# Two joints of an attention and mixture-of-experts kernel: the last batches' weight traffic and key copies, and the first gather of the expert block

## The chip, the cores and the metric

The program runs on one core of a Trainium2 chip. A time is the device time of one execution in microseconds (us). The profile is one more execution, recorded by the hardware profiler: every time inside it counts from the start of its span. TensorE is called PE here, VectorE DVE, ScalarE ACT, GpSimd POOL, and SyncE SP. SP computes nothing; it issues transfers. ACT and POOL can issue transfers too.

## What is computed

A layer with cross-attention (32 batches of 112 tokens, 512 channels, 16 heads, 375 context rows) and a mixture of 8 experts, of which each token takes its best 2. Cut to what matters:

```python
x = x + xattn(layernorm(x), ctx, mask, ...)         # q and output projections on int8-rounded operands
h = layernorm(x)
probs = softmax(h @ router_w.T); vals, idx = top_k(probs, 2); vals = vals / vals.sum(-1)
for e in range(8):                                  # 3584 tokens, hidden width 352
    gate, up = split(h @ gate_up[e].T); y = silu(gate) * up @ down[e].T
    out += combine[:, e] * y
return x + out
```

## The kernel before, in words

Three blocks run one after another, and all engines meet at a barrier between them.

**Attention** (lines 18 to 912). Iteration `it` computes the scores and softmax of batch `it`, head by head (h = 0 to 15), and beside them prepares batch n = it + 1 (keys, values, queries), finishes batch m = it - 1, and stores batch m2 = it - 2. The order on each engine is written out by hand in a `body(it, ...)` for that engine. Iterations 3 to 28 are a hardware loop; -1 to 2 and 29 to 33 are written out. Iteration 31 (B - 1) is the last with scores; it has no next batch to project, so PE has little to do there. Iteration 32 (`late`) finishes batch 31, iteration 33 stores it.

Keys and queries must be copied into "stacks" (`k_stack`, `q_stack`) before PE can use them. SP issues these copies: 12 for heads 8 to 15 (`stack_keys(1)`, at the start of an iteration, after the last score of the one before), 12 for heads 0 to 7 of the next batch (`stack_keys(0)`), then 12 for its queries. In iterations 0 to 2 two of the 12 copies of `stack_keys(0)` are issued by ACT instead (`ACT_KEYS`).

In each iteration one of 32 slices of the expert weights is split in a high and a low part, so that the expert block can load them: SP loads the slice into `w_raw` (lines 197 and 198, after the four stores of the slice before have landed: `w_stored`), ACT makes the high part `w_hi` after the softmax of head 12 (line 439), POOL makes the low part in place (`w_lo`, line 329), and SP stores both (lines 245 and 246, four transfers) at the end of its iteration. All of these are in the tile `w_raw_hi`.

In iterations 31 and 32 DVE also does the routing of the first 30 batches (lines 496 to 700), between the heads.

**Routing** (`route`). A long chain on DVE ends in `gather` (line 1124) and `scatter` (line 1126): for each of 63 tiles of 128 slots the rows of `h2` to be gathered and where their results go. Meanwhile SP loads expert 0 (`load_expert`, 8 transfers, 4.3 MB), writes a zero block and stores the weights by token (`weights_by_token`); it waits for both before it leaves the block.

**Experts** (`experts`). For each tile t POOL copies a column of `gather` to `gather_idx` (line 1233), gathers 128 rows of `h2` with an indirect transfer (line 1237), gathers the weights of the tokens (`cw_rows`, line 1250), and later scatters the results (line 1245). PE transposes the rows of tile t + 1 (line 1348) and multiplies them by the expert's weights (lines 1324 and 1357). SP loads expert 1, then counts `weights_ready` up for expert 0, and so on. PE waits for `weights_ready` before the first product of a tile.

## Time and profile before

| | |
|---|---|
| median of 3 runs | 1551.54 us (1551.52 to 1556.08) |
| the profiled execution | 1553.85 us |
| its span | 1552.1 us |
| PE busy | 1484.4 us, 96% of the span |
| DVE, ACT, POOL busy | 889.0, 881.5, 635.5 us |

In the page's 40 slices of the span (38.8 us each) PE is busy for nine tenths or more in all but the first, the last, and slices 28 and 29. Those two hold the end of attention, the routing block and the start of the experts. A row of the timeline gives the start, the duration, the engine with the line, what was written from what, and in brackets how long the engine had sat idle and what released it. An engine name with q (SPq, POOLq, ACTq) is the queue of instructions that issue transfers or count.

### The profile page before, as it was taken

How to read it: one execution, taken by the hardware profiler on the slowest of the kernel's cores; microseconds unless marked ns; L12 is line 12 of the kernel's file. 1: busy time of each engine (PE TensorE's matmuls, PEld its weight loads, DVE VectorE, ACT ScalarE, POOL GpSimd, SP SyncE). 2: the span in 40 equal slices, each digit the busy share in tenths (PEclk: the TensorE clock that was granted, in tenths of full speed). 3: DMA queues.
4: the chain of work that ended last, by engine and by line, in shares of the span. 5: the costliest groups of instructions: out<-in, count | busy, mean ns of one | idle time of the engine just before them, and what ended most of it. 6: DMA issues, size and time to landing. Idle time of an engine off the chain costs nothing. (4 is left out here: it accounts for less than half of the span.)

```text
span 1552.1 us, 40193 instructions
## 1 busy us (share of the span) xinstructions
PE 1484.4 (96%) x11596; PEld 1310.6 (84%) x11597; DVE 889.0 (57%) x2402; ACT 881.5 (57%) x2100; POOL 635.5 (41%) x663
## 2 busy tenths in 40 slices
PE   6999999999999999999999999995599999999996
PEld 5888888888888888888888888874599999999995
DVE  7667766667766676676766667668422222222221
ACT  4776767776777776776777776663133333333332
POOL 3234333344333433334333343323255555656553
PEclk9999999999999999999999999996699999999998
DMA  8676677776777767777677766763647775574743
GB/s 265 180 208 181 179 207 213 214 190 183 218 202 211 188 181 216 202 210 191 182 217 202 214 188 183 204 171 127 215 78 189 189 193 145 123 186 82 189 79 48
DMA packets 220123, 281.08 MB, mean 181 GB/s; under 512 B 83568, under 2 KB 164976, under 8 KB 220080
## 3 DMA queue, kind: packets, MB, share of 16 engines
q1 hardware_dynamic: 202608, 246.32, 56.4%
q0 software_dynamic: 16128, 33.30, 11.7%
q10 hardware_dynamic: 1344, 0.92, 0.3%
q8 instruction: 23, 0.38, 0.1%
q14 instruction: 20, 0.16, 0.0%
HBM read 118.31 MB, written 66.17 MB: 119 GB/s over the span
## 5 line engine op out<-in xcount | busy, mean ns | idle before, releaser
L362 ACT ACTIVATE probs<-probs,neg_max 112x375 f32<-112x375 f32 x512 | 312.1, 610 | 197.2 <-DVE neg_max L536 191.9
L536 DVE CUSTOM_DVE_ANT_0 probs<-score,neg_mask 112x375 f32<-112x375 f32 x504 | 275.3, 546 | 228.0 <-PE score L749 223.3
L757 PE MATMUL turn<-ident,probs 112*125 112x112 f32 x1536 | 262.8, 280 | 3.7 <-ACT probs_t L349 2.6
L349 ACT ACTIVATE probs_t<-turn 125x336 f32<-125x336 f32 x512 | 225.7, 441 | 68.1 <-PE turn L757 67.5
L757 PEld LDWEIGHTS turn<-ident,probs 112*125 112x125 f32 x1536 | 225.9, 189 | 36.0 <-issue 15.7
L749 PE MATMUL score<-k_stack,q_stack 96*112 96x376 f32 x496 | 200.6, 404 | 3.8 <-DMA q_stack<-q_lo 2.0
L304 POOL TENSOR_TENSOR q_tok<-q_tok,bq_row 112x512 f32<-112x512 f32 x32 | 41.8, 1306 | 361.7 <-DVE q_tok L643 361.7
L791 PE MATMUL proj<-ctx_hi,wk_hi 128*128 128x376 f32 x512 | 176.5, 345 | 10.7 <-DVE ctx_lo L714 10.5
L791 PE MATMUL proj<-ctx_lo,wk_hi 128*128 128x376 f32 x512 | 171.9, 336 | 0.0
L791 PE MATMUL proj<-ctx_hi,wk_lo 128*128 128x376 f32 x512 | 171.4, 335 | 0.0
L1287 DVE TENSOR_TENSOR a_lo<-a_ps,a_hi 128x384 fp32r<-128x384 f32 x63 | 35.2, 558 | 237.8 <-ACT a_hi L1262 218.6
L796 PE MATMUL proj<-wv_hi,ctx_hi 128*125 128x512 f32 x384 | 151.6, 395 | 0.0
L796 PE MATMUL proj<-wv_hi,ctx_lo 128*125 128x512 f32 x384 | 151.2, 394 | 0.0
L796 PE MATMUL proj<-wv_lo,ctx_hi 128*125 128x512 f32 x384 | 151.1, 394 | 0.0
L1245 POOL DMA_INDIRECT out<-y_rows,scatter_idx x63 | 101.8, 1616 | 79.3 <-issue 30.0
L324 POOL TENSOR_TENSOR ctx_lo<-ctx_stage,ctx_hi 128x1504 fp32r<-128x1504 f32 x31 | 106.6, 3437 | 38.0 <-ACT ctx_hi L434 37.6
L329 POOL TENSOR_TENSOR w_raw_hi<-w_raw_hi 128x1056 fp32r<-128x1056 f32 x32 | 78.9, 2465 | 88.7 <-ACT w_raw_hi L439 88.7
L791 PEld LDWEIGHTS proj<-ctx_hi,wk_hi 128*128 128x128 f32 x512 | 97.1, 190 | 17.5 <-ACT ctx_hi L447 10.1
L1275 ACT ACTIVATE y_rows<-y_ps,row_share 128x512 f32<-128x512 f32 x63 | 43.4, 689 | 106.9 <-PE y_ps L1357 61.8
L791 PEld LDWEIGHTS proj<-ctx_lo,wk_hi 128*128 128x128 f32 x512 | 97.5, 191 | 0.0
L791 PEld LDWEIGHTS proj<-ctx_hi,wk_lo 128*128 128x128 f32 x512 | 96.7, 189 | 0.0
L362 ACT ACTIVATION_READ_ACCUMULATOR probs<-probs,neg_max 112x1 f32 x512 | 95.6, 187 | 0.0
(244 smaller groups left out, 3339.2 us busy)
## 6 DMA issues: line engine op xcount, KB each, us to landing
k_stack<-x_and_k SPq DMA_DIRECT2D x762, 94.0 KB, 2.4
ctx_stage<-ctx_t SPq DMA_DIRECT2D x32, 750.0 KB, 5.1
q_stack<-q_hi SPq DMA_DIRECT2D x250, 56.0 KB, 2.0
w_raw_hi<-gate_up_t SPq DMA_DIRECT2D x32, 352.0 KB, 3.1
gate_up_dram_hi<-w_raw_hi SPq DMA_DIRECT2D x32, 352.0 KB, 5.3
gate_up_dram_lo<-w_raw_hi SPq DMA_DIRECT2D x32, 352.0 KB, 5.6
gate_up_hi<-gate_up_dram_hi SPq DMA_DIRECT2D x16, 704.0 KB, 4.8
gate_up_lo<-gate_up_dram_lo SPq DMA_DIRECT2D x16, 704.0 KB, 9.6
```

The lines of the kernel that those rows point to most:

```text
L304: pool.tensor_tensor(q_tok[:, :], q_tok[:, :], W["bq_row"][0:N, :], ALU.add).then_inc(q_biased, 1)
L324: pool.tensor_tensor(c_lo[:, par % 2, :, :], stage[:, :, :], c_hi[:, par % 2, :, :].bitcast(F32), ALU.subtract).then_inc(c_lo_made, 1)
L329: pool.tensor_tensor(w_lo[:, :], w_raw[:, :], w_hi[:, :].bitcast(F32), ALU.subtract).then_inc(w_lo_made, 1)
L349: act.activation(probs_t[:, h % RING_T, :, :], turn[h % 2][0:LC, 0:LT * N].rearrange("p (l n) -> p l n", l=LT), ACT.Copy).then_inc(turned_ ...
L362: act.activation(probs[:, h % DS, :], probs[:, h % DS, :], ACT.Exp, bias=neg_max[:, par % 2, h:h + 1], scale=-1.0, accum_out=total[:, par ...
L536: dve.tensor_tensor_reduce(probs[:, h % DS, :], (last_score[h % 4] if last else score[h % 2])[0:N, 0:L], neg_mask[:, p, :], 1.0, BIG, ALU. ...
L749: pe.matmul(score[h % 2][0:N, 0:LP], q_st[:, par % 2, h, :], k_st[:, h, :], start=True, stop=True).then_inc(scored, 1)
L757: mm = pe.transpose(turn[h % 2][0:LC, l * N:(l + 1) * N], probs[:, h % DS, l * LC:(l + 1) * LC], W["ident"][0:N, 0:N])
L791: mm = pe.matmul(bank[:, 0:LP], W[w][:, t, 128 * u:128 * u + 128], c[:, q, t, :], start=(t == 0 and w == "wk_hi" and c is c_hi), stop=(t = ...
L796: mm = pe.matmul(bank[0:LC, :], c[:, q, t, l * LC:(l + 1) * LC], W[w][:, t, :], start=(t == 0 and w == "wv_hi" and c is c_hi), stop=(t == ...
L1245: pool.indirect_dma_start(out, bass.IndirectOffsetOnAxis(ap=si[par][:, 0:1], axis=0), y[:, par, :], None, compute_op=ALU.add).then_inc(sca ...
L1275: act.activation(y[:, other, :], y_ps[other][:, 0:C], ACT.Copy, scale=share[:, other:other + 1]).then_inc(y_made, 1)
```

## The change

1. ACT issues its two key copies in iterations 29 and 30 as well.
2. SP's four weight stores of iteration 30 move from the end of iteration 30 to the middle of iteration 31, behind the key copies, and the last slice's load follows them. Its `w_lo` on POOL moves from iteration 31 to iteration 32, behind the reciprocal root of batch 30, and its four stores to the same iteration, behind the load of `x_res`.
3. POOL copies the indices of tile 0 and issues its row gather inside the routing block, as soon as `gather` is made.
4. In the experts block SP waits for the row gathers of tiles 0 and 1 before it issues expert 1's load.
5. In the routing block SP issues the store of `weights_by_token` before it waits for the zero block.

```diff
@@ SP, attention @@
                     stack_keys(1)
-                    need(sp, w_stored, 64 * it)
-                    sp.dma_start(w_raw[:, 0:WG], W["gate_up_flat"][:, bass.ds(it * WG, WG)]).then_inc(w_in, 16)
-                    sp.dma_start(w_raw[:, WG:WG + WD], W["down_flat"][:, bass.ds(it * WD, WD)]).then_inc(w_in, 16)
+                    if inside or it < B - 1:
+                        load_weights(it)
...
+                if not inside and it == B - 1:
+                    store_weights(B - 2)
+                    load_weights(B - 1)
+                if not inside and it == B:
+                    store_weights(B - 1)
...
-                    stack_keys(0, ACT_KEYS if not inside and 0 <= it < 3 else ())
+                    stack_keys(0, ACT_KEYS if not inside and (0 <= it < 3 or it >= B - 3) else ())
...
-                if has_a:
...
+                if has_a and (inside or it < B - 2):
+                    store_weights(it)
@@ POOL, attention @@
+                if not inside and it == B:
+                    pool.wait_ge(ln2, 3 * m2 + 3)
+                    pool.wait_ge(w_hi_made, B)
+                    pool.wait_ge(w_stored, 64 * (B - 1))
+                    pool.tensor_tensor(w_lo[:, :], w_raw[:, :], w_hi[:, :].bitcast(F32), ALU.subtract).then_inc(w_lo_made, 1)
...
-                if has_a:
+                if has_a and (inside or it < B - 1):
@@ ACT, attention @@
-                    if h == 8 and has_a and has_n and not inside and it < 3:
+                    if h == 8 and has_a and has_n and not inside and (it < 3 or it >= B - 3):
@@ POOL, routing @@
+            pool.wait_ge(gather_made, 1)
+            pool.tensor_copy(R["gather_idx"][0][:, :], R["gather"][:, 0:1]).then_inc(R["gi_set"], 1)
+            pool.wait_ge(R["gi_set"], 1)
+            pool.sem_inc(R["go"], 1)
+            pool.indirect_dma_start(R["rows"][:, 0, :], None, h2, bass.IndirectOffsetOnAxis(ap=R["gather_idx"][0][:, 0:1], axis=0)).then_inc(R["rows_in"][0], 16)
@@ SP, routing @@
-            sp.wait_ge(pad_written, 16)
             sp.wait_ge(cw_steps, 4)
             sp.dma_start(weights_by_token.rearrange("(b n) e -> n b e", n=N), cw[:, :, :]).then_inc(stored, 16)
+            sp.wait_ge(pad_written, 16)
             sp.wait_ge(stored, 16)
@@ SP, experts @@
+            for par in range(2):
+                sp.wait_ge(rows_in[par], 16)
             load_expert(sp, R, 1)
@@ POOL, experts @@
-                if exists(t + 2, inside):
+                if exists(t + 2, inside) and (inside or t > -2):
```

`load_weights` and `store_weights` hold the removed load and the four stores of lines 245 and 246, with their waits.

The queue of SP where iteration 30 ends and 31 begins. Before:

```order
L245 DMA gate_up_dram_hi<-w_raw_hi 128x704 [waits w_lo_made]
L246 DMA down_dram_hi<-w_raw_hi 128x352
L245 DMA gate_up_dram_lo<-w_raw_hi 128x704
L246 DMA down_dram_lo<-w_raw_hi 128x352
L184 DMA k_stack<-x_and_k 32x2x376 [waits unit_out,scored]
L184 DMA k_stack<-x_and_k 32x2x376 x11
L197 DMA w_raw_hi<-gate_up_t 128x704 [waits w_stored]
L198 DMA w_raw_hi<-down_t 128x352
L204 DMA out<-y_h 112x512 [waits x1_steps]
```

The same place after, where `out`, `h2_rows` and `x_res` are the rows of batches 29 and 30:

```order
L184 DMA k_stack<-x_and_k 32x2x376 [waits unit_out,scored]
L184 DMA k_stack<-x_and_k 32x2x376 x11
L214 DMA out<-y_h 112x512 [waits x1_steps]
L216 DMA h2_rows<-y_h 112x512 [waits ln2]
L219 DMA x_res<-x 112x512 [waits x1_steps]
L195 DMA gate_up_dram_hi<-w_raw_hi 128x704 [waits w_lo_made]
L196 DMA down_dram_hi<-w_raw_hi 128x352
L195 DMA gate_up_dram_lo<-w_raw_hi 128x704
L196 DMA down_dram_lo<-w_raw_hi 128x352
L189 DMA w_raw_hi<-gate_up_t 128x704 [waits w_stored]
L190 DMA w_raw_hi<-down_t 128x352
```

The key copies now stand ahead of the four stores, and the load of the last slice stands behind them.

POOL's instructions in iterations 31 and 32. Before:

```order
L308 TENSOR_TENSOR x_res<-x_res,bo_row 112x512 [waits x1_steps,x_res_ld]
L329 TENSOR_TENSOR w_raw_hi<-w_raw_hi 128x1056 [waits w_stored,w_hi_made]
L287 TENSOR_TENSOR y_h<-y_h,x_res 112x512 [waits ln2,x1_steps,o_out]
L290 TENSOR_SCALAR var_eps2<-mv2 112x1 [waits ln2]
L292 TENSOR_TENSOR rstd2<-var_eps2,minus_half 112x1 [waits rstd2_made]
L308 TENSOR_TENSOR x_res<-x_res,bo_row 112x512 [waits x1_steps,x_res_ld]
```

After:

```order
L325 TENSOR_TENSOR x_res<-x_res,bo_row 112x512 [waits x1_steps,x_res_ld]
L299 TENSOR_TENSOR y_h<-y_h,x_res 112x512 [waits ln2,x1_steps,o_out]
L302 TENSOR_SCALAR var_eps2<-mv2 112x1 [waits ln2]
L304 TENSOR_TENSOR rstd2<-var_eps2,minus_half 112x1 [waits rstd2_made]
L309 TENSOR_TENSOR w_raw_hi<-w_raw_hi 128x1056 [waits w_stored,w_hi_made,ln2]
L325 TENSOR_TENSOR x_res<-x_res,bo_row 112x512 [waits x1_steps,x_res_ld]
```

The low part moved behind three small instructions of iteration 32.

POOL where the routing block (its last row of work is `cw`) ends. Before:

```order
L1004 TENSOR_TENSOR cw<-cw,second_share 112x256 [waits cw_steps]
L944 UNCONDITIONAL_BRANCH
L1227 UNCONDITIONAL_BRANCH [waits barrier_Pool_Activation_PE_DVE_SP_gather]
L1233 COPY gather_idx0<-gather 128x1
L1237 DMA rows<-h2_rows,gather_idx0 128x512 [waits gi_set]
L1250 DMA cw_rows<-weights_by_token,gather_idx0 128x8
L1233 COPY gather_idx1<-gather 128x1
L1237 DMA rows<-h2_rows,gather_idx1 128x512 [waits gi_set]
```

After:

```order
L1021 TENSOR_TENSOR cw<-cw,second_share 112x256 [waits cw_steps]
L1024 COPY gather_idx0<-gather 128x1 [waits gather_made]
L1027 DMA rows<-h2_rows,gather_idx0 128x512 [waits gi_set]
L961 UNCONDITIONAL_BRANCH
L1253 UNCONDITIONAL_BRANCH [waits barrier_Pool_Activation_PE_DVE_SP_gather]
L1276 DMA cw_rows<-weights_by_token,gather_idx0 128x8
L1259 COPY gather_idx1<-gather 128x1
L1263 DMA rows<-h2_rows,gather_idx1 128x512 [waits gi_set]
```

The first copy and the first row gather now stand ahead of the barrier.

SP at the start of the experts block, after the change; before, the first row has no wait and the rest is the same:

```order
L1175 DMA gate_up_hi<-gate_up_dram_hi 128x2x704 [waits rows_in1,rows_in0]
L1175 DMA gate_up_hi<-gate_up_dram_hi 128x2x704
L1175 DMA down_hi<-down_dram_hi 128x2x512
L1175 DMA down_hi<-down_dram_hi 96x512
L1175 DMA gate_up_lo<-gate_up_dram_lo 128x2x704 x2
L1175 DMA down_lo<-down_dram_lo 128x2x512
L1175 DMA down_lo<-down_dram_lo 96x512
L1246 TENSOR_LOAD last_tile [waits expert_loaded0_0,expert_loaded0_1,expert_loaded1_0,expert_loaded1_1]
```

All eight issues of expert 1 stand behind both gathers, and the count of `weights_ready` for expert 0 stands behind these issues.

## Rows read from the trace of the kernel before

**Rows 1.** Busy time by stretch: length, PE, PEld, DVE, ACT, POOL; granted clock, DMA.

```profile
1060.00:1080.00 20.00, 11.69 (x89) 8.26 (x89) 16.34 (x41) 2.73 (x6) 4.36 (x6) 0.55 0.31 101
1165.00:1230.00 65.00, 65.00 (x391) 61.09 (x390) 18.43 (x38) 21.43 (x39) 37.59 (x48) 1.00 0.80 211
```

**Rows 2.** Timeline, PE, the stalls at the end of attention.

```profile
1003.98 0.40 PE L749 MATMUL score<-k_stack,q_stack 96*112 96x376 f32 x1 [1.57 <-issue]
...
1046.50 0.65 PE L739 MATMUL score<-k_stack,q_stack 96*112 96x376 f32 x1 [1.71 <-DMA k_stack<-x_and_k]
...
1060.46 0.55 PE L757 MATMUL turn<-ident,probs 112*125 112x112 f32 x3 [1.31 <-ACT probs_t L349]
```

**Rows 3.** Timeline, SP's queue, iterations 29 to 31.

```profile
985.00 9.74 SPq L184 DMA_DIRECT2D k_stack<-x_and_k  x12
...
1001.86 0.60 SPq L222 DMA_DIRECT2D q_stack<-q_lo  x1
...
1034.80 0.36 SPq L245 DMA_DIRECT2D gate_up_dram_hi<-w_raw_hi  x1
...
1036.75 8.15 SPq L184 DMA_DIRECT2D k_stack<-x_and_k  x12
...
1047.01 0.42 SPq L209 DMA_DIRECT2D x_res<-x  x1
```

**Rows 4.** Timeline, ACT, POOL and DVE in iteration 31, each engine apart.

```profile
1054.95 1.07 ACT L439 ACTIVATE w_raw_hi<-w_raw_hi 128x1056 fp32r<-128x1056 f32 x1
...
1059.28 0.61 ACT L362 ACTIVATE probs<-probs,neg_max 112x375 f32<-112x375 f32 x1 [1.08 <-DVE neg_max L536]
...
1056.09 2.42 POOL L329 TENSOR_TENSOR w_raw_hi<-w_raw_hi 128x1056 fp32r<-128x1056 f32 x1 [3.64 <-ACT w_raw_hi L439]
...
1046.18 0.40 DVE L505 TENSOR_TENSOR ctx_stage<-ctx_stage,prio 112x240 f32<-112x240 f32 x1
...
1052.43 0.69 DVE L675 TENSOR_TENSOR o_tok<-misc,inv_total 112x512 f32<-112x512 f32 x1 [0.96 <-PE misc L817]
...
1056.79 1.99 DVE L505 TENSOR_TENSOR ctx_stage<-ctx_stage,prio 112x240 f32<-112x240 f32 x1
```

**Rows 5.** The slices' transfers by tile, iterations 29 to 31: issue to landing.

```profile
DMA to landing us min/median/max: 2.3/3.0/3.4
```

**Rows 6.** Timeline, POOL and DVE in iteration 29.

```profile
998.65 2.47 POOL L329 TENSOR_TENSOR w_raw_hi<-w_raw_hi 128x1056 fp32r<-128x1056 f32 x1 [2.59 <-ACT w_raw_hi L439]
...
1000.82 0.58 DVE L459 TENSOR_SCALAR x_and_k<-x_and_k,x_inv 112x512 f32<-112x512 f32 x1
```

**Rows 7.** Timeline, DVE, SP, POOL and PE around the start of the experts.

```profile
1098.81 0.22 DVE L1124 SCALAR_TENSOR_TENSOR gather<-slot_ps,upper 128x64 int32<-128x64 f32 x1
...
1099.32 0.28 DVE L1126 SCALAR_TENSOR_TENSOR scatter<-empty,pad_row,gather 128x64 int32<-128x64 f32 x1
...
1100.52 0.90 SPq L1151 DMA_DIRECT2D gate_up_hi<-gate_up_dram_hi  x2
...
1103.76 1.03 SPq L1151 DMA_DIRECT2D down_lo<-down_dram_lo  x2
...
1101.76 1.24 POOL L1237 DMA_INDIRECT rows<-h_rows,gather_idx  x1 [1.01 <-POOL gather_idx L1233]
...
1105.26 0.97 POOL L1237 DMA_INDIRECT rows<-h_rows,gather_idx  x1 [0.82 <-POOL gather_idx L1233]
...
1108.05 1.11 PE L1348 MATMUL h_ps<-ident,rows 128*128 128x128 f32 x4 [10.25 <-DMA rows<-h_rows,gather_idx]
...
1110.84 0.66 PE L1324 MATMUL gate_ps<-gate_up_hi,h_hi 128*128 x1 [1.68 <-DVE h_lo L1290]
```

**Rows 8.** A gather with no load beside it; rates in 0.125 us steps from 1120.

```profile
1120.20 0.97 POOL L1237 DMA_INDIRECT rows<-h_rows,gather_idx  x1 [0.84 <-POOL gather_idx L1233]
...
GB/s 4 0 0 0 0 0 0 0 0 0 0 0 0 0 66 197 131 98 66 229 360 459 426 66 0 0 0 0 0 0 0 0 0 0 0 0 0 0 12 15
```

**Rows 9.** The page's transfer issues: tile, queue, count, KB each, us to landing.

```profile
gate_up_dram_lo<-w_raw_hi SPq DMA_DIRECT2D x32, 352.0 KB, 5.6
```

More of the change, by code:

```diff
@@ L185, in stack_keys, with load_weights, store_weights @@
                                      src[rows, 2 * half:2 * half + 2, :].bitcast(F32)).then_inc(k_stacked[half], 16)
+            def load_weights(it):
+                need(sp, w_stored, 64 * it)
+                sp.dma_start(w_raw[:, 0:WG], W["gate_up_flat"][:, bass.ds(it * WG, WG)]).then_inc(w_in, 16)
+                sp.dma_start(w_raw[:, WG:WG + WD], W["down_flat"][:, bass.ds(it * WD, WD)]).then_inc(w_in, 16)
+            def store_weights(it):
+                need(sp, w_lo_made, it + 1)
+                for src, gate_up_part, down_part in ((w_hi, "gate_up_hi", "down_hi"), (w_lo, "gate_up_lo", "down_lo")):
+                    sp.dma_start(W[gate_up_part][:, bass.ds(it * WG, WG)], src[:, 0:WG].bitcast(F32)).then_inc(w_stored, 16)
+                    sp.dma_start(W[down_part][:, bass.ds(it * WD, WD)], src[:, WG:WG + WD].bitcast(F32)).then_inc(w_stored, 16)
             def body(it, par, inside=False):
@@ L931, in most_tiles, with route @@
     return (2 * tokens + E * (SLOTS - 1) + E - 2) // SLOTS
-def route(nc, W, R, weights_by_token, pad_rows):
+def route(nc, W, R, h2, weights_by_token, pad_rows):
     N, B = W["tokens"], W["batches"]
@@ L981, in route @@
         tile_made, numbered, row_made = sem("at_tile_made"), sem("at_tile_numbered"), sem("at_row_made")
-        numbers_made = sem("numbers_made")
+        numbers_made, gather_made = sem("numbers_made"), sem("gather_made")
         zero = sb("zero", [128, pad_rows.shape[1]])
@@ L1123, in _ @@
             link(dve.tensor_scalar(upper[:, :], slot_ps[:, 0:NTP], 0.0, None, ALU.is_gt))
-            link(dve.scalar_tensor_tensor(R["gather"][:, :], slot_ps[:, 0:NTP], float(T // 2), upper[:, :], ALU.add, ALU.subtract))
+            dve.scalar_tensor_tensor(R["gather"][:, :], slot_ps[:, 0:NTP], float(T // 2), upper[:, :], ALU.add, ALU.subtract).then_inc(gather_made, 1)
+            dve.wait_ge(gather_made, 1)
             link(dve.tensor_scalar(empty[:, :], slot_ps[:, 0:NTP], 0.0, None, ALU.is_equal))
@@ L1174, in experts @@
         gate_ps, up_ps, y_ps = [[bank(f"{n}_ps{i}") for i in range(2)] for n in ("gate", "up", "y")]
-        rows, cw = sb("rows", [128, 2, C]), sb("cw_rows", [128, 2, E])
-        gi, si = [sb(f"gather_idx{i}", [128, 1], I32) for i in range(2)], [sb(f"scatter_idx{i}", [128, 1], I32) for i in range(2)]
+        rows, cw = R["rows"], sb("cw_rows", [128, 2, E])
+        gi, si = R["gather_idx"], [sb(f"scatter_idx{i}", [128, 1], I32) for i in range(2)]
         share = sb("row_share", [128, 2])
@@ L1406, in program @@
              "loaded": [[ctx.enter_context(nc.semaphore(f"expert_loaded{e}_{turn}")) for e in range(E)] for turn in range(2)],
-             "weights_ready": ctx.enter_context(nc.semaphore("weights_ready"))}
+             "weights_ready": ctx.enter_context(nc.semaphore("weights_ready")),
+             "rows": sb("rows", [128, 2, C]), "gather_idx": [sb(f"gather_idx{i}", [128, 1], I32) for i in range(2)],
+             "gi_set": ctx.enter_context(nc.semaphore("gi_set")), "go": ctx.enter_context(nc.semaphore("go")),
+             "rows_in": [ctx.enter_context(nc.semaphore(f"rows_in{par}")) for par in range(2)]}
         for part in ("hi", "lo"):
@@ L1411, in program @@
             R[f"down_{part}"] = sb(f"down_{part}", [128, 2 * FT * C], F32R)
-        route(nc, W, R, weights_by_token, out[T:T + PAD_ROWS, :])
+        route(nc, W, R, h2, weights_by_token, out[T:T + PAD_ROWS, :])
         experts(nc, W, R, h2, weights_by_token, out)
```

8 lines of the change are left out of this document (2 added, 6 removed).

## The prediction

> **What bounds the kernel now.** First I read the busy time by stretch. In the experts' steady part PE is busy all the time at full clock from 1165 to 1230 [rows 1], and batches 1 to 28 look the same on the page. A transfer that starts earlier there brings nothing. In the 20 us from 1060 it is busy for 11.69 us at a granted clock of 0.55 [rows 1]: there the end is set by waits. So I went to the timeline of that end, and to the start of the experts, where PE sits idle for 10.25 us until the first gather has landed [rows 7]. Only these two places can pay. Five waits matter: two for key and query copies [rows 2, 3], one on DVE beside POOL's low part [rows 4], the first gather, and a count that SP gives [rows 7].
>
> **Part 1, ACT's two key copies.** The first score of iteration 30 comes 1.57 us late [rows 2]. The row names no releaser; what its code waits for is the last query copy, issued at 1001.86 to 1002.46 [rows 3], about 2 us ahead of it. SP had issued without a pause since 985.00: 12 key copies in 9.74 us, 0.81 each, then the queries. Two copies fewer give 1.6 us, so the stall goes nearly whole: **-1.55 us** (from 0, if the queries aren't made in time, to -1.6). On ACT the two issues stand ahead of the softmax of head 8, in a stretch in which PE has other work; I take them at nothing. If that cover is gone they cost the time of two such issues on SP, up to 1.6 us per iteration. Iteration 31 starts without a stall before, so the copies saved in iteration 30 gain nothing themselves; they keep SP ahead.
>
> **Part 2, keys ahead of the stores.** SP issues four stores from 1034.80 to 1036.75 and then the 12 key copies [rows 3]. After the change these wait only for the last score of iteration 30, which PE ends at about 1035.0. So they start 1.7 us earlier, and the stall of 1.71 us at head 8 [rows 2] goes. DVE does not gain all of that at once, since it has routing work in between. But the next thing that it waits for is PE again: at 1052.43 it had idled 0.96 us for PE's transpose [rows 4], which follows five slow pairs of scores and transposes. I follow the chain without the stall to there: 1.6 us earlier.
>
> Then ACT rounds the last slice, after head 12 (1054.95, so 1053.3 now) [rows 4]. Its load has moved behind the stores. In the time of before: the key copies end at 1043.2, three small issues at 1044.6, four stores (1.95 us, as at 1034.80) at 1046.6; the last of them lands up to 3.4 us after its issue at 1046.1, at 1049.5; the load's two issues, 1.1 us apart at their ends, land 3.0 to 3.4 us later: 1053.2 to 1053.6 [rows 3, 5]. ACT waits 0 to 0.3 us. Queued behind it are the copies of transposed probabilities that PE waits for. I take 0.2.
>
> **Part 3, the low part moved.** DVE's product at 1056.79 took 1.99 us; the same line took 0.40 us at 1046.18. It ran beside POOL's low part, which ended at 1058.51, and ended 0.3 us after it [rows 4]. Without POOL beside it, it is 1.6 us shorter. Head 15's scores then reach ACT earlier, but ACT would only be free at 1058.1 instead of 1059.28 [rows 4]: 1.2 us gained of the 1.6. Together with part 2: 1.6 - 0.2 + 1.2 = 2.6 us, of which PE's stall of 1.31 us at 1060.46 [rows 2] is the visible end. The rest of the chain (outputs, normalisation, router) shifts as it is. **-2.6 us** (from -1.2 to -3.3).
>
> In its new place the low part stands behind the root of batch 30 and ahead of the addition to `x_res`, whose load lands later than the 2.4 us that it takes, so I count nothing. DVE beside it first does reductions and one product from PSUM; its scaling to integers starts 2.6 us after the low part may start. Rows show what an overlap costs: beside POOL's 998.65 to 1001.12, such a scaling started at 1000.82 and took 0.58 us [rows 6], a tenth more than elsewhere. The Trainium skill (SBUF — State Buffer, "Who interferes with whom") says that a DVE instruction with two SBUF inputs, or in a 2-port mode, contends with GpSimd for a shared port pair, and that the loser blocks whole. By that rule the product of 1.99 us is explained, and it speaks against the new place: a scaling caught there would wait for POOL's end, which from 1000.82 would be 0.3 us and not 0.1; the sum would lose 0.2 us at most. The measured row decides.
>
> The four last stores are issued at about 1068, and the next instruction on SP waits until some 1073 anyway: nothing.
>
> **Part 4, the first gather.** `gather` is made at 1099.03 [rows 7]. Before, POOL copied at 1100.57 and issued 1.19 us later. Now: copy at 1099.1, issue at 1100.3, done at 1101.5, landed 2.8 us after its start (a gather with nothing beside it: issued at 1120.20, the rate is zero again from 1123.0 [rows 8]), at 1103.1, against 6.24 us beside expert 1's load. So PE's transposes come at about 1103.1 instead of 1108.05. That is the promise: 4.9 us.
>
> But the block can't end before POOL has ended, at 1101.5; DVE ended at 1099.60 before. The experts started up to 0.92 us after that [rows 7]; I take 0.4, since SP was itself still waiting for its store: start at 1101.9 instead of 1100.52. The second gather stood 4.74 us behind the start; less the copy and gather that moved out (1100.57 to 1103.00) 2.3: issued at 1104.2, landed at 1107.0. Only now does SP issue expert 1's eight transfers, 4.27 us (1100.52 to 1104.79) [rows 7]: 1111.3. And only **behind these** does it count `weights_ready` up for expert 0, whose weights have long been there. PE needs that count for its first product, which stood at 1110.84. It now stands at about 1111.35: **+0.5 us** (0 to +1.3, by the 0.92 and slower landing). The gather's 4.9 us turn into a wait for SP. The load itself is not needed until tile 7 or 8, some 45 us later. It now ends at about 1122 instead of 1115, beside the gather of tile 3 (issued at 1120.20, needed 6.8 us later, while a contended one takes 6.24): nothing, barely.
>
> **Part 5**, the store of weights ahead of the wait: the block's end is now POOL's, so it gains nothing itself.
>
> **Sum.** -1.55 - 2.6 + 0.5 = -3.65 us. Against the profiled execution (1553.85 us, span 1552.1) that is 1550.2; against the median of 1551.54 it is **1547.9 us**. The profiled one took 2.3 us more than the median; if one of the stalls was only there, less is gained.
>
> **Rivals.**
> *PE's clock stays up in attention.* It fell at the stall of 1046.50 (the score took 0.65 us instead of 0.40) and stood at 0.55 from 1060 [rows 1, 2]. There PE is busy 11.69 us, about half of it on the chain. At full clock these instructions take about 0.6 of their time: 2 us more gained, total -5.7, 1545.9. For it: one stall is gone. Against it: the idle time after 1060 stays. The opposite, a clock that rises later in the experts after the longer idle time, costs up to 1.4 us, an estimate: half of the 2.8 us that lay between the transposes and the first product (1108.05 to 1110.84) [rows 7], if the clock's rise counted from the transposes.
> *The wait for SP doesn't bind*, so that the gather's 4.9 us arrive: -1.55 - 2.6 - 4.9 = -9.0, 1542.5. Against it stands the order of SP's instructions.
> *The last slice comes late*, and this is the one that ends slower. ACT waits after head 12 for the load, which waits for four stores. Each us past 1053.3 is lost one for one. Over all iterations the larger of these stores landed after 5.6 us in the median [rows 9], against 3.0 here [rows 5]. With that the load lands 2.2 us later and the total is -1.5: 1550.0. From 3.65 us more than forecast, a landing at 1057.2, the whole is slower than before; 6 us over makes 1553.9. SP is otherwise idle there, which speaks against it.
> *The change does nothing*: the stalls were those of the profiled execution alone: +0.5 from the experts, 1552.
>
> **How the numbers follow.** A measurement can tell about 0.3% (4.65 us) from no change. The forecast with its bounds (1546.9 to 1549.5) gets 0.54, the clock rival 0.22, the gather arriving 0.06, the late slice below the point of loss or no stalls 0.14, slower by more than 0.3% 0.04. All of the gather's and most of the clock's share lie under 1546.9, and a little of the forecast's by its gains' upper bounds: faster 0.32, same 0.64, slower 0.04. The range leaves out the arriving gather and the worst of the late slice: 1545.0 to 1551.2.
>
> **What would show it.** Right: no idle time at the first score of iteration 30, under 0.3 us at head 8 of iteration 31, 0.4 us for the product of line 505, the transposes of tile 0 at some 9 us behind `gather` before and 4 now, and then an idle PE for 7 us until SP's last issue of expert 1. Wrong: a first product less than 10 us behind `gather` (it was 11.8), ACT waiting over 1 us for the last slice, or new idle time at tile 3.

## The result, and the profile after

The changed kernel takes **1555.68 us** (median of 14 runs, 1554.33 to 1558.47) against 1551.53 us before (14 runs, 1550.05 to 1556.08): a ratio of 1.0024, 95% interval 1.0017 to 1.0032 (3.7 us by the ratio, 4.15 by the medians). It is slower by some 4 us, where 1547.9 was forecast and 1551.2 was the upper end of the range. The profiled execution took 1558.47 us with a span of 1556.8, against 1553.85 and 1552.1 before.

Marks at which both kernels do the same, in us of the two profiled executions, show where the time came in:

| mark | before | after | difference |
|---|---|---|---|
| ACT rounds slice 28 | 965.26 | 967.02 | +1.8 |
| ACT rounds slice 29 | 997.50 | 999.26 | +1.8 |
| ACT rounds slice 30 | 1031.17 | 1031.42 | +0.3 |
| first reduce of the routing block | 1080.28 | 1080.82 | +0.5 |
| start of DVE's instruction that makes `gather` | 1098.81 | 1099.34 | +0.5 |
| first product of the experts | 1110.84 | 1115.28 | +4.4 |
| last product of the experts | 1539.38 | 1544.32 | +4.9 |

The first 1.8 us stood there before iteration 29, where nothing was changed; over the executions of all kernels below slice 28 was rounded at 964.5 to 967.1, whatever their attention code, so that much is scatter. Of the rest three things are to be read. Of the 4.15 us forecast for the attention, 1.5 came between slices 29 and 30 and nothing behind slice 30. The experts start 3.9 us later behind `gather` (15.94 us from the start of that instruction to the first product, instead of 12.03). And another 0.5 us is lost between the first product and the last.

The prediction counts from the end of that instruction, at 1099.03 before; everything here counts from its start, which is 0.22 us more. The start of the experts scatters too: over seven executions with the code of before it is 11.59 to 12.03 us, 11.7 in the mean.

The start of the experts after the change, timeline rows of POOL, DVE, PE and SP (start, duration, engine and line; in brackets the idle time before it and its releaser); they answer to [rows 7]:

```profile
1099.34 0.22 DVE L1147 SCALAR_TENSOR_TENSOR gather<-slot_ps,upper 128x64 int32<-128x64 f32 x1
...
1100.82 1.24 POOL L1027 DMA_INDIRECT rows<-h_rows,gather_idx  x1 [1.01 <-POOL gather_idx L1024]
1105.44 0.94 POOL L1276 DMA_INDIRECT cw_rows<-weights_by_token,gather_idx  x1 [3.38 <-POOLq L961]
1107.41 0.97 POOL L1263 DMA_INDIRECT rows<-h_rows,gather_idx  x1 [0.83 <-POOL gather_idx L1259]
...
1104.79 0.11 DVE L1307 MEMSET a<- 128x64 f32 x1 [4.65 <-PEq L961]
...
1105.05 1.09 PE L1374 MATMUL h_ps<-ident,rows 128*128 128x128 f32 x4 [6.72 <-DVE a L1307]
1115.28 0.66 PE L1350 MATMUL gate_ps<-gate_up_hi,h_hi 128*128 x1 [9.15 <-SPq L1251]
...
1110.78 0.90 SPq L1175 DMA_DIRECT2D gate_up_hi<-gate_up_dram_hi  x2
...
1114.02 0.97 SPq L1175 DMA_DIRECT2D down_lo<-down_dram_lo  x2
```

POOL had issued the first gather by 1102.06, but nothing of the experts block runs before 1104.79: DVE's first instruction there had idled 4.65 us, and its releaser is line 961, the end of the routing block. Line 1251, which PE waits for, is SP's count of `weights_ready`; it stands behind the load whose last row ends at 1114.99.

The end of attention after the change, rows of POOL, DVE, ACT and PE:

```profile
1045.39 0.64 PE L756 MATMUL score<-k_stack,q_stack 96*112 96x376 f32 x1
...
1048.49 1.32 POOL L325 TENSOR_TENSOR x_res<-x_res,bo_row 112x512 f32<-112x512 f32 x1 [7.07 <-DMA x_res<-x]
...
1048.71 1.37 DVE L614 SCALAR_TENSOR_TENSOR ctx_stage<-v,logits 112x240 f32<-112x240 f32 x1
...
1056.32 0.40 DVE L522 TENSOR_TENSOR ctx_stage<-ctx_stage,prio 112x240 f32<-112x240 f32 x1
...
1055.37 1.08 ACT L456 ACTIVATE w_raw_hi<-w_raw_hi 128x1056 fp32r<-128x1056 f32 x1 [0.80 <-DMA w_raw_hi<-down_t]
...
1058.60 1.91 PE L920 MATMUL misc<-wo_int,o_int_t 128*112 128x512 bf16 x4
...
1060.55 0.75 DVE L565 SCALAR_TENSOR_TENSOR y_h<-misc,o_scale,wo_row 112x512 f32<-112x512 f32 x1 [2.16 <-PE misc L920]
```

The product of line 505 (522 now) takes the forecast 0.40 us instead of 1.99 [rows 4], and in this execution no score waits for key copies any more: the first of head 8 stands 14.0 us behind the rounding of slice 30, where it stood at 15.3. But it already runs at half clock (0.64 us), and at DVE's `o_tok` (20.5 us behind that rounding, 21.3 before) only 0.7 us are left. DVE's multiply-add of line 614 runs beside POOL's addition and takes 1.37 us. ACT waits 0.80 us for the last slice, whose rounding now stands 23.95 us behind that of slice 30 instead of 23.78. And the four output matmuls take 1.91 us where they took 1.03 before. The granted clock fell there. It is the third number from the end in the view of busy time by stretch, where 1.00 is TensorE's upper level (2.4 GHz) and 0.50 its lower (1.2 GHz). After:

```profile
1058.00:1062.00 4.00, 3.77 (x15) 2.79 (x15) 1.33 (x4) 2.41 (x8) 0.62 (x1) 0.59 0.01 2
```

Before:

```profile
1058.00:1062.00 4.00, 2.35 (x32) 1.71 (x34) 3.79 (x14) 2.02 (x6) 1.33 (x2) 1.00 0.67 250
```

### The profile page after: what moved, and what is told of

It reads as the page before. It is cut to its first block and busy times, and to the rows that moved or that the text cites. A ratio compares the mean times of both kernels' runs of the same rounds, so it can differ in the third digit from the quotient of the medians.

```text
span 1556.8 us, 40196 instructions
## 1 busy us (share of the span) xinstructions
PE 1485.7 (95%) x11596; PEld 1311.3 (84%) x11597; DVE 886.6 (57%) x2402; ACT 881.2 (57%) x2100; POOL 635.4 (41%) x663
## 5 line engine op out<-in xcount | busy, mean ns | idle before, releaser
L1271 POOL DMA_INDIRECT out<-y_rows,scatter_idx x63 | 101.8, 1617 | 83.3 <-POOL scatter_idx L1266 25.3
L1350 PE MATMUL gate_ps<-gate_up_hi,h_hi 128*128 x252 | 87.9, 349 | 9.1 <-SPq L1251 9.1
```

Of the source, the lines that this page charges most:

```text
L1271: pool.indirect_dma_start(out, bass.IndirectOffsetOnAxis(ap=si[par][:, 0:1], axis=0), y[:, par, :], None, compute_op=ALU.add).then_inc(sca ...
L1350: mm = pe.matmul(ps[:, 0:F], h[:, par, 128 * k:128 * k + 128], R[w][:, bass.ds(place * (KT * F2) + (k * F2 + i * F), F)], start=(k == 0 an ...
```

## The experiments

All medians stand beside runs of the kernel before on the same chip, with medians from 1551.12 to 1551.78 us. "Behind `gather`" is the time from the start of DVE's instruction that makes the table to the first product, 12.03 us in the profiled execution of before. Part 5 was in no run by itself.

**1. Only the gather (parts 3 to 5 of the change), and only the attention (parts 1 and 2).** Each is the changed kernel with the other functions of the kernel before.

> Parts 3, 4 and 5 of the change alone (first gather in the routing block, expert 1's load behind two gathers, store of weights first); attention as before. Theory: the routing block does not end before the gather has landed, and SP counts expert 0 in only behind expert 1's issues, so the first product stands 15.7 us behind the making of gather, as in the changed kernel (11.8 before): about 3.9 us slower than before, 1555.4. Rival, that the loss is in attention: about the time of before, 1551.5 to 1552.

Measured 1557.25 us (ratio 1.0042, 1.0028 to 1.0056); 16.27 us behind `gather`, 4.2 more than before. That is 1.9 us short of the 6.1 by the medians; 10 finds 1.3 of them.

> Parts 1 and 2 alone (ACT's two key copies in iterations 29 and 30, stores behind the keys, last low part in iteration 32); routing and experts as before. Theory: the stall of 1.5 us at iteration 30 goes, iteration 31 and what follows takes as long as in the changed kernel (+0.3): 1.2 us faster than before, 1550.3. Rival, that attention carries the loss (the loop's 4th and 5th iterations took 2 us more in the changed kernel's trace): 1552 to 1553, and the same 2 us there again.

Measured 1550.6 us (0.9995, 0.9986 to 1.0004); 11.83 us behind `gather`. So the loss is wholly in the experts' start and what follows it, and the attention's 4.15 us of forecast are at most 2.2 (the interval's end), 0.8 by the ratio and 0.5 by the medians.

**2. The changed kernel with expert 0 counted first.**

```diff
-            for par in range(2):
-                sp.wait_ge(rows_in[par], 16)
-            load_expert(sp, R, 1)
             for e in range(E):
+                if e == 1:
+                    for par in range(2):
+                        sp.wait_ge(rows_in[par], 16)
+                    load_expert(sp, R, 1)
```

> The changed kernel, with SP counting weights_ready up for expert 0 before it waits for the two gathers and issues expert 1's load. Theory: the 9.15 us wait of PE for SP goes, the first product follows the transposes of tile 0 by 2.8 us and stands at about 8.3 us behind gather: 7.4 us faster than the changed kernel, about 1548.5. Rival, that another wait stands right behind it (rows of tile 1 or 2 under expert 1's load): less than 4 us of it, 1552 or more.

Measured 1549.87 us (0.9991, 0.9982 to 1.0000); 8.51 us behind `gather` instead of 15.94. SP's order alone keeps PE from a product for 7.4 us. The median is 1.4 us above the expected one: the rows of tile 3 came 0.63 us late, and the loop is slower than in before (10).

**3. The gather in the routing block, expert 1's load issued there too.** Attention as before; SP's two waits and the load at the start of the experts block are gone.

```diff
+            load_expert(sp, R, 1)
+            sp.wait_ge(pad_written, 16)
             sp.wait_ge(stored, 16)
```

> Parts 3 and 5 alone, with expert 1's load issued in the routing block right behind the store of weights, so that the first gather runs beside it and lands late while POOL's issue stays where it is. Theory, the block's end waits for the landing of POOL's gather: the experts start 0.2 to 0.5 us after a landing that comes some 5 to 6 us after the issue, so 7 us or more behind gather. Rival, a fixed cost of leaving the block after POOL has issued (2.5 us from the end of the issue, as in the changed kernel): the experts start 5.2 us behind gather, whatever the landing.

Measured 1554.2 us in the one profiled execution, so the trace is what counts here. POOL, and the view of the tile `rows` (issue to landing, least, median, most: two gathers):

```profile
1100.62 1.24 POOL L1010 DMA_INDIRECT rows<-h_rows,gather_idx  x1 [1.01 <-POOL gather_idx L1007]
1108.57 0.94 POOL L1257 DMA_INDIRECT cw_rows<-weights_by_token,gather_idx  x1 [6.71 <-POOLq L944]
...
DMA to landing us min/median/max: 3.3/5.1/6.9
```

The gather beside the load landed 6.9 us behind its issue, at 1107.5, and the experts block began then: POOL idled 6.71 us for the block's end, against 3.38 in the changed kernel, where it landed after 3.6. The exit of the block follows the **landing** of POOL's gather: in this kernel, the changed one, the gather kernel of 1, kernel 2 and the last of 10, DVE's first instruction of the experts stands some 0.4 us behind it, with landings of 3.6 to 6.9 us. SP's load isn't waited for in that way: its last transfers, issued from 1098.67, landed 10.5 us later, at 1109.2 or after, when the experts were running. A kernel with that load in flight at the exit and no gather wasn't run, so that the load itself delays the exit a little isn't excluded.

**4. SP's new order without the gather in the routing block.** The kernel before, with expert 0 counted first and expert 1's load behind the rows of tiles 0 and 1 (the edit of 2).

> The kernel before with one edit: SP counts expert 0's weights first, then waits until the rows of tiles 0 and 1 have landed, and only then issues the load of expert 1. Both gathers stay in the experts block. In before the first gather was issued at 1101.76 us beside the load of expert 1 (issues 1100.5 to 1104.8) and its transposes began at 1108.05, 6.3 us later; in the changed kernel, with nothing of SP's beside them, gathers landed 3.3 to 3.6 us behind their issue. Theory (the load in flight is what delays the gather, and the first product waits for nothing else): the first product 2.4 to 2.9 us earlier, at about 1108.2 instead of 1110.84, the median 1551.5 - 2.6 = 1548.9. Rival A (the gather's landing doesn't depend on the load beside it): first product at 1110.8, 1551.5. Rival B (expert 1's weights, now issued some 8 us later, come late for the first tile of expert 1): a new idle time of PE before that tile that eats the gain, 1551.5 or more.

Measured 1549.47 us (0.9980, 0.9971 to 0.9989); 8.91 us behind `gather`. PE:

```profile
1105.12 1.11 PE L1351 MATMUL h_ps<-ident,rows 128*128 128x128 f32 x4 [7.12 <-DMA rows<-h_rows,gather_idx]
1107.92 0.65 PE L1327 MATMUL gate_ps<-gate_up_hi,h_hi 128*128 x1 [1.69 <-DVE h_lo L1293]
```

The transposes wait 7.12 us for the gather instead of 10.25 [rows 7]. So the promise of the change is real, 3.1 us of it against the execution of before (2.8 against the mean of the seven): the gather landed after 3.4 us, where it takes 6.2 to 6.5 beside the load in the kernels that leave the order as it was. The rows of tile 3, whose gather now runs beside the load, came 0.22 us late.

**5. The changed kernel's order without its gather.** As 4, but load first and count behind it.

```diff
+            for par in range(2):
+                sp.wait_ge(rows_in[par], 16)
             load_expert(sp, R, 1)
             for e in range(E):
```

> The kernel before with one edit: SP waits until the rows of tiles 0 and 1 have landed, then issues the load of expert 1, and only then counts expert 0's weights (the changed kernel's order); both gathers stay in the experts block. It takes SP's order by itself. Theory: the second gather lands at about 1108.4 as where expert 0 was counted first, SP's 8 issues take 4.2 us, the first product starts at 1112.9 instead of 1107.9 there and 1110.84 in before, 14 us behind the table of the gather; median 1549.5 + 5 = 1554.5. The changed kernel had 15.9 us there, so the gather in the routing block would cost the other 1.9 us. Rival (PE's later start is made good where tile 1 and expert 1 wait anyway): first product at 1112.9, but the median under 1553.

Measured 1553.54 us (1.0015, 1.0006 to 1.0024); 13.92 us behind `gather`. The order costs 5.0 us against 4, as expected. The changed kernel's other 2.0 us (15.94) are its later second gather, issued 8.07 us behind `gather` instead of 6.02, because the routing block ended late.

**6. The load behind the rows of tile 0 alone.** Against the kernel of 4:

```diff
-                    for par in range(2):
-                        sp.wait_ge(rows_in[par], 16)
+                    sp.wait_ge(rows_in[0], 16)
                     load_expert(sp, R, 1)
```

> The kernel before with SP's new order, but the load of expert 1 waits for the rows of tile 0 alone. The first gather has the DMAs for itself, the second, issued at about 1105.1, goes beside the load (issues from about 1105.3). Theory (a gather beside the load lands some 5 to 7 us after its issue instead of 3.3, and tile 1 isn't needed before that): first product at 1107.9, rows of tile 1 by 1111, no idle time for them, median 1549.5 as with both awaited. Rival (tile 1's transposes come late): idle time of PE at tile 1, up to 2 us, 1551.5.

Measured 1549.15 us (0.9990, 0.9981 to 0.9999); 8.95 us behind `gather`, and no idle time at tiles 1 and 2, though their gathers took 5.8 and 6.6 us.

**7. The parts of the attention.** First the keys alone (part 1):

```diff
-                    stack_keys(0, ACT_KEYS if not inside and 0 <= it < 3 else ())
+                    stack_keys(0, ACT_KEYS if not inside and (0 <= it < 3 or it >= B - 3) else ())
```

> The kernel before with part 1 alone: in the last three iterations ACT issues two of its key copies. The prediction took the idle 1.57 us ahead of the score at 1003.98 us of before as SP's late key copies, and gave 1.55 us to this edit: median 1551.6 - 1.55 = 1550.0. Rival (that idle time belongs to the one profiled execution: in four others with the old split, 29 to 30 took 32.13 to 32.56 us instead of 33.67): w_hi of iteration 29 to 30 takes 32.1 us, and the median is that of before, 1551.6, or 0.3 us below for the shorter wait at 1046.50.

Measured 1551.79 us (0.9998, 0.9989 to 1.0007). Rounding of slice 29 to 30: 32.17 us. Over the executions of all kernels with the old key code it is 32.1 to 32.6 us in six and more in three: 33.67 (before), 33.37 (5) and 33.06 (10), where the same score had waited 1.57, 1.27 and 0.96 us (and 0.40 in kernel 3, with 32.56). With the new code it is 32.1 to 32.2 in all eight. The stall [rows 2] is an occasional one. PE's row in the kernel of 5:

```profile
1004.84 0.40 PE L749 MATMUL score<-k_stack,q_stack 96*112 96x376 f32 x1 [1.27 <-issue]
```

Then the low part alone:

```diff
+                if not inside and it == B:
+                    pool.wait_ge(ln2, 3 * m2 + 3)
+                    pool.wait_ge(w_hi_made, B)
+                    pool.wait_ge(w_stored, 64 * (B - 1))
+                    pool.tensor_tensor(w_lo[:, :], w_raw[:, :], w_hi[:, :].bitcast(F32), ALU.subtract).then_inc(w_lo_made, 1)
...
-                if has_a:
+                if has_a and (inside or it < B - 1):
```

> The kernel before with the low part of the last slice (and its stores) moved to iteration 32 alone; loads and stores of slice 30, and the keys, stay as in before. It isolates DVE's product of line 505, which took 1.99 us in before beside POOL's subtraction at 1056.09. Theory of the prediction (the subtraction blocks the product and the product stands on the path): the product takes 0.40 us, the stretch from ACT's w_hi of iteration 30 to the first reduce of the routing block 1.2 us shorter than the 49.1 of before, median 1550.3. Rival (the path behind it, PE's granted clock or the next product, takes the place): the product takes 0.40 us and the stretch stays at 49 us or more, 1551.5.

Measured 1550.88 us (0.9995, 0.9986 to 1.0004); the product took 0.41 us, the stretch from slice 30 to the routing block's first reduce 48.21 us instead of 49.11. From the rounding of slice 31 it took 24.13 us instead of 25.33: the 1.2 us that part 3 had forecast.

Then the load of `x_res` behind the four stores of slice 30 (in the kernel with parts 1 and 2):

```diff
+                if not inside and it == B - 1:
+                    store_weights(B - 2)
                 if has_m:
                     need(sp, x1_steps, 2 * m)
                     sp.dma_start(x_res[:, :], x[m, :, :]).then_inc(x_res_ld, 16)
                 if not inside and it == B - 1:
-                    store_weights(B - 2)
                     load_weights(B - 1)
```

> The kernel before with parts 1 and 2 of the change (keys by ACT; stores of slice 30 ahead of the keys, low part of 31 moved), but with the load of x_res in iteration 31 behind the stores of slice 30 instead of ahead of them. In the changed kernel POOL's addition of x_res at 1048.49 met DVE's multiply-add at 1048.71, which took 1.37 us instead of 0.41. Theory (the addition that came earlier eats 1 us of the gain): no such meeting, multiply-add 0.41 us, the stretch from w_hi of iteration 30 to the routing block 47.9 us where that of the changed kernel was 49.4, and the median 0.5 to 1 us under that of parts 1 and 2 alone (1550.6), about 1550.0. Rival (what decides is where the stretch of half clock falls, not the addition): the stretch takes 47.9 or 49.4 us by that alone, and the median stays at 1550.6.

Measured 1550.5 us (0.9995, 0.9986 to 1.0004), the median of parts 1 and 2 alone. The stretch took 47.52 us, the multiply-add 0.41. The same stretch over all executions:

| attention code | slice 30 to 31 | 31 to routing | both, us | multiply-add, us | output matmuls, us |
|---|---|---|---|---|---|
| old (nine kernels, among them before and those with the keys or the buffers alone) | 23.2 to 24.1 | 25.3 in five, 25.9 in three, 26.98 once | 49.1 to 49.5, once 50.48 | 0.41 | 1.03 in the five, 1.32 to 1.71 in the others |
| low part alone | 24.08 | 24.13 | 48.21 | 0.41 | 1.03 |
| parts 1 and 2, in after and in 2 | 23.95, 23.90 | 25.45, 25.46 | 49.40, 49.36 | 1.37, 0.41 | 1.91, 1.91 |
| parts 1 and 2, alone and in 8 | 23.71, 24.05 | 24.17, 24.16 | 47.88, 48.21 | 0.41, 1.36 | 1.03, 1.03 |
| the same, `x_res` behind (7; 9; last of 10) | 23.36, 23.41, 23.68 | 24.16, 24.17, 24.16 | 47.52, 47.58, 47.84 | 0.41 | 1.03 |

Four executions with the same code fall into two groups, and the groups go by the output matmuls, that is by PE's clock, not by the multiply-add: the theory of this experiment fell, its rival fits. The whole difference lies behind slice 31, 1.3 us, and the old code shows the same there: 25.3 us where the output matmuls took 1.03 us, 25.9 or more where they took longer. The multiply-add took 0.41 us in kernels 1 (attention) and 2 although it ran beside POOL's addition there too; it had started first, and the addition took 1.34 and 1.35 us instead of 1.27. The meeting costs 0.3 us of the stretch at most (48.21 against 47.88). With `x_res` behind three executions of three are fast; whether that is its doing or chance, so few don't tell.

**8. Attention and SP's order together**, the first gather left in the experts block.

> Parts 1 and 2 of the change in the attention (which alone gave 1550.6), and SP's new order in the experts (expert 0 counted first, rows of tiles 0 and 1 awaited, then the load of expert 1), the first gather left in the experts block. If both are additive: 1550.6 - 2.6 = 1548.0, and 1.9 us below the changed kernel with expert 0 counted first (1549.9), because the routing block no longer waits for a gather. Rival (the gather in the routing block is worth as much as its landing costs there): the same 1549.9. Rival B (late weights of expert 1): 1550.6 or more.

Measured 1548.11 us (0.9977, 0.9968 to 0.9986).

**9. The same with `x_res` behind.**

> Parts 1 and 2 of the change in the attention, with the load of x_res in iteration 31 behind the stores of slice 30, and SP's new order in the experts (expert 0 counted first, rows of tiles 0 and 1 awaited, then the load of expert 1), the first gather in the experts block. Theory (gains add up): attention and SP's order gave 1548.1, the stretch from w_hi of iteration 30 to the routing block was 47.5 us with x_res behind against 48.2 there: 1547.6. Rival (the 0.7 us of that stretch is scatter between executions): 1548.1 or a little more.

Measured **1547.52 us** (0.9975, 0.9964 to 0.9987), 8.94 us behind `gather`. It beats both kernels, by some 4 us and (across chips) 8; from 1548.11 it can't be told apart. In 8 the rows of tile 3 came 0.63 us late, here 0.24.

**10. The steady part.** The timelines show no idle time of PE from 1130 to 1500 in any kernel, and yet the transposes of one tile and the next lay 6.76 us apart in kernels 1 (gather) and 3 and after the change, 6.77 in 2, and 6.72 to 6.75 (6.737 in the mean) in before and in all others of 1 to 9. The rows of the fifth tile and of the last, 58 tiles on, before:

```profile
1133.71 0.60 PE L1348 MATMUL h_ps<-ident,rows 128*128 128x128 f32 x4
...
1524.61 0.60 PE L1348 MATMUL h_ps<-ident,rows 128*128 128x128 f32 x4
```

And after:

```profile
1137.29 0.60 PE L1374 MATMUL h_ps<-ident,rows 128*128 128x128 f32 x4
...
1529.47 0.60 PE L1374 MATMUL h_ps<-ident,rows 128*128 128x128 f32 x4
```

390.90 us against 392.18: 1.3 us. The change also moved two allocations: `rows` (4096 bytes of each partition) and two `gather_idx` (4 bytes each) now stand ahead of the experts' weights. Three kernels test that. The first moves the allocations and no instruction:

```diff
+             "rows": sb("rows", [128, 2, C]), "gather_idx": [sb(f"gather_idx{i}", [128, 1], I32) for i in range(2)],
...
-        rows, cw = sb("rows", [128, 2, C]), sb("cw_rows", [128, 2, E])
+        rows, cw = R["rows"], sb("cw_rows", [128, 2, E])
```

> The kernel before with one edit, which moves no instruction: rows and gather_idx are allocated outside the experts' function, ahead of the weights' buffers, as in the changed kernel. Theory (the weights' shifted addresses cost PE's reads): the transposes of one tile and the next lie 6.76 us apart instead of 6.735, first to last product 1.3 us longer, median 1551.5 + 1.3 = 1552.8. Rival (the gather in the routing block or its order causes it): 6.735 us a tile, 1551.5.

Measured 1553.28 us (1.0011, 1.0002 to 1.0020). The fifth tile and the last:

```profile
1133.06 0.60 PE L1348 MATMUL h_ps<-ident,rows 128*128 128x128 f32 x4
...
1525.39 0.60 PE L1348 MATMUL h_ps<-ident,rows 128*128 128x128 f32 x4
```

392.33 us: the layout does it, without any instruction moved. The transposes, which read `rows`, take 273 ns in the mean in both kernels; among the products that read the weights some got longer (`gate_ps` 345 to 347 ns on `gate_up_hi` and `h_hi`, 323 to 326 on `gate_up_lo`), which speaks for the weights' place and against that of `rows`. Kernel 2 has the same layout and 6.773 us a tile; its other 0.013 us, 0.8 in the whole loop, stay open. The second gives each index 64 bytes:

> As the kernel with only the buffers moved, but each gather_idx takes 64 bytes of a partition instead of 4, so that the weights lie 4224 bytes further instead of 4104. Theory (the odd 8 bytes do it): 6.735 us a tile, 1551.5. Rival (any move of the buffers does it, or the layout doesn't matter at all): 6.76 us a tile and 1552.8, or 6.735 in both kernels.

Measured 1553.26 us (1.0006, 0.9997 to 1.0015); the steps alternate between 6.735 and 6.77, 6.753 in the mean, and the fifth tile and the last lie 391.95 us apart. So the odd 8 bytes are not the whole of it, and what else in the addresses counts stays open. The two medians are the same and can't tell 0.4 us. The third is the changed kernel with the edit of 2, with `x_res` behind the stores, and with the allocations behind the weights again:

```diff
-             "rows": sb("rows", [128, 2, C]), "gather_idx": [sb(f"gather_idx{i}", [128, 1], I32) for i in range(2)],
...
             R[f"down_{part}"] = sb(f"down_{part}", [128, 2 * FT * C], F32R)
+        R["rows"], R["gather_idx"] = sb("rows", [128, 2, C]), [sb(f"gather_idx{i}", [128, 1], I32) for i in range(2)]
```

> The changed kernel with three edits: expert 0 counted before SP's waits and load of expert 1, x_res of iteration 31 behind the stores, and rows and gather_idx allocated behind the weights. Theory (the layout and SP's order were what the gather in the routing block cost, its late exit is made good by its earlier issue): first product 8.5 us behind the table of the gather (8.9 with both gathers in the experts block), 6.735 us a tile, tile 3's rows 0.6 us late, median within 0.5 us of 1547.5, the same version without the gather in the routing block. Rival (the gather itself slows the loop): 6.76 us a tile, 1548.8 or more.

Measured 1547.86 us (0.9976, 0.9967 to 0.9985), 8.51 us behind `gather`, 6.737 us a tile. From 9, which has the gather behind the block (1547.52), it can't be told apart; the intervals are 1.4 and 1.8 us each way.

## Why the prediction was wrong

**Part 1** (-1.55): the step that failed is the reading of one stall in one execution as a standing cost. ACT's copies do remove it, but it comes in three of nine executions of the old code, and a short one (0.40) in a fourth, so the edit is worth about 0.5 us in the mean (the four waits over nine, an estimate) and less in a median. The warning was in the text, the profiled execution was 2.3 us above the median, and the rival "the change does nothing" had this mechanism; but the forecast took the stall whole.

**Part 3** (-1.2 of the -2.6) was right: the product takes 0.40 us, and the way from the last slice's rounding to the routing block fell from 25.3 us to 24.1 or 24.2 in six executions, the one with the low part alone among them. In the changed kernel's own execution this was lost again, and the step that failed there was to hold the clock fixed: where it stood at half just when the output matmuls ran (1.91 us instead of 1.03), the same way took 25.45 us. The rival on the clock had the opposite sign, and its reading that the clock fell at the stall of 1046.50 doesn't hold: without that stall it fell too, and head 8's first score took 0.64 us. What puts the fall there isn't settled; a mean over executions decides this term, not one trace.

**Part 2** (-1.4 of the -2.6): the step that failed is the chain from the stall to ACT's rounding of the last slice. The key copies start 1.75 us earlier, as forecast. The chain was to be 1.6 us ahead at `o_tok` and is 0.7 in after (0.6 in the mean of the seven kernels with parts 1 and 2 against the other ten), and the rounding was to come 1.4 us earlier and comes no earlier at all with the stores where the change has them (23.7 to 24.1 us behind slice 30, against 23.2 to 24.1), and 0.3 us earlier with `x_res` behind. One part of it is the load of the last slice. It was to land by 1053.6 in the time of before and landed at about 1055.1: the last store was issued 0.5 us later than forecast and took 4.3 us to land instead of 3.4, and the load's second transfer took up to 3.8 us from its issue. ACT waited 0.80 us for it in after, 0.93 in 2, 0.2 to 0.6 in four executions and not at all in the last of 10, where 0.2 were forecast. What holds the chain up ahead of `o_tok` stays open.

A smaller step was missing in both parts: the load of `x_res` was moved too, since it stands behind the key copies, and its addition on POOL came at 1048.49 instead of 1051.18 and met the multiply-add (0.96 us longer, of which 0.3 at most are on the path). The page of the Trainium skill that the prediction weighed (SBUF — State Buffer, "Who interferes with whom") fits both meetings, 1.99 and 1.37 us instead of 0.41. Its rule was applied to the instruction that was moved by hand and not to the one that moved with it.

**Part 4** (+0.5): the mechanism was right, and it was the main one: the transposes came early, at 5.7 us behind `gather` instead of 9.2, and PE then waited 9.15 us until SP had issued the load and counted. The size was off by two steps. "The block can't end before POOL has ended" was taken as the end of POOL's row; the block ended when the gather had **landed**, and the experts' first instruction stands at 1104.79, 5.4 us behind `gather`, where 1101.9, 3.1 us behind it, was forecast. The Trainium skill (Perfetto Trace Analysis, "DMA Instruction — SWDGE (GPSIMD)") states that such a row ends when the descriptors are written and not when the data have moved; the trace agrees, with 1.24 us for the row and 3.6 to the landing. Then every landing was taken at 2.8 us and measured 3.3 to 3.7. Worked again with these: gather 2 issued 1107.41, landed 1110.7, eight issues to 1115.0, product at 1115.28: +3.9 behind `gather` where 0.5 was forecast. Of the 3.4 us between them the exit has 2.3, the second landing 0.6, and small steps the rest. The bound of +1.3 rested on the same step. The price of the whole is what SP's order costs (5.0 us in 5) less the 3.1 us that the free gather gives, plus 2.0 for the late exit.

**Not priced**: the moved allocations, +1.3 us in the trace (1.6 in the median, with an interval of 1.4 each way). I had read them as no instruction's business.

**Sum as measured**: +3.9 at the start of the experts, +0.5 from the first product to the last, and -0.8 in the attention (the ratio of 0.9995 of parts 1 and 2 alone) give +3.6, against +3.7 by the ratio and +4.15 by the medians. The +0.5 are the +1.3 of the loop less 0.9 from the first product to the fifth tile (22.0 us instead of 22.9), which is scatter: it is 21.9 to 22.9 over seven executions with the start of before. The bounds of the prediction's own terms add up to 1546.6 to 1551.6; the narrower 1546.9 to 1549.5 that its chances use isn't worked out there. The rival that was to end on the slower side, a late last slice, cost at most 0.7 us of ACT's waiting more than forecast; the loss came from the place for which a loss was written down and bounded too low. New idle time at tile 3 did not come after the change, where PE was late itself; it did in 2, 4, 8 and 9 (0.63, 0.22, 0.63 and 0.24 us), so "nothing, barely" was a little too good.

## What to carry to other kernels

An instruction at the end of a block is priced with everything the block's exit waits for; ask of an asynchronous transfer whether the exit waits for its landing, and move it only where that is covered. When a transfer is put behind a wait, look first at what the same queue counts for others: here one line in another place turned +4 into -1.4 us. A stall or a clock phase of one profiled execution is a cost only if a second execution shows it, and an allocation that moves is a part of the change like any other.

## What the runs showed of the hardware

- The exit of a block waits for the landing of GpSimd's indirect transfer (3.38 us of idle POOL with a landing of 3.6, 6.71 with 6.9; the first instruction behind it some 0.4 us after the landing in five kernels), and not for that of SyncE's plain ones, which landed 10.5 us behind their issue, after the exit.
- A gather of 128 rows of 2 KB took 3.3 to 3.7 us to land with nothing beside it at the start of the experts, 5.0 to 5.8 us when a load of 4.3 MB began within 0.3 us behind it, and 6.2 to 7.4 us in the midst of that load.
- The place of the weights in SBUF changed the pace of the matmuls on them (the transposes of `rows`, which moved too, kept theirs), at full clock and without any wait: 6.737 us a tile, 6.753 with the weights 4224 bytes further in each partition, 6.760 with 4104.
- Where a DVE product or multiply-add on two SBUF tiles met a POOL instruction that had started first, it took 1.99 and 1.37 us instead of 0.41. Where it had started first itself, it took 0.41 and POOL's addition 1.35 instead of 1.27.
